# Attention scores of two light items formed in one block of matmuls, in every second slot

## What is computed

```python
# light: 8 heads of 64, windows of 64 tokens that see the window before and the window after
sim = jnp.einsum('bhnid,bhnjd->bhnij', qw * scale, kk)
sim = jnp.where(valid[None, None, :, None, :], sim, neg)
attn = jax.nn.softmax(sim, axis=-1)
lo = jnp.einsum('bhnij,bhnjd->bhnid', attn, vv)
# heavy: 256 routed queries against 256 routed keys, the same 8 heads
hsim = jnp.einsum('bhid,bhjd->bhij', hq * scale, hk)
hattn = jax.nn.softmax(hsim, axis=-1)
return light_out + heavy_out
```

## Time and profile before

| | |
|---|---|
| median of 3 runs | 2064.11 us (2062.43 to 2066.58) |
| the profiled execution's own time | 2061.01 us |
| its span, first to last instruction | 2059.2 us |
| mean granted clock of TensorE | 0.977 |
| PE busy | 1875.1 us (91%) |
| DVE busy | 1388.5 us (67%) |
| ACT busy | 1203.6 us (58%) |
| POOL busy | 1172.0 us (57%) |

### The profile page before, as it was taken

One profiled execution on the slowest core, in us unless ns is written; L12 is line 12 of the kernel. 1 busy time (PEld: TensorE's weight loads), 2 busy tenths in 40 slices (PEclk: granted clock), 3 DMA queues, 4 the chain that ended last, 5 costly groups with the idle time before them and its releaser, 6 DMA issues.

```text
span 2059.2 us, 38092 instructions
## 1 busy us (share of the span) xinstructions
PE 1875.1 (91%) x11764; PEld 1398.7 (68%) x11764; DVE 1388.5 (67%) x4771; ACT 1203.6 (58%) x2974; POOL 1172.0 (57%) x1356
## 2 busy tenths in 40 slices
PE   3488899889989989989989989989999999999998
PEld 1166678656656666666666666666666788888887
DVE  5355457756855865875874875775754488888887
ACT  5487567565565565565566566566555555555554
POOL 3999852662772782782682683583453444444444
PEclk8599999999999999999999999999999999999999
DMA  6688887200310310310310220220121111111110
GB/s 200 248 267 289 275 267 251 67 27 1 100 40 1 98 42 1 95 45 1 93 47 1 81 55 5 77 57 8 37 63 82 38 42 42 42 42 42 36 38 21
DMA packets 103841, 168.15 MB, mean 82 GB/s; under 512 B 13249, under 2 KB 64857, under 8 KB 102745
## 3 DMA queue, kind: packets, MB, share of 16 engines
q1 hardware_dynamic: 80600, 112.91, 16.8%
q0 software_dynamic: 20736, 52.52, 8.1%
q10 hardware_dynamic: 2304, 0.28, 0.1%
HBM read 80.33 MB, written 85.34 MB: 80 GB/s over the span
## 4 chain that ended last, share of the span: by engine, by line
PE 51%; DVE 16%; POOL 10%; issue 10%; ACT 9%; DMA 4%; ACTq 0%; SPq 0%; DVEq 0%; POOLq 0%
PE bank L730 7%; PE bank L732 6%; PE bank L731 6%; PE bank L1022 4%; PE bank L1011 4%; PE bank L982 4%; PE bank L993 4%; PE bank L953 3%; PE bank L890 2%; ACT prob L1319 2%; PE bank L872 2%; POOL prob L2005 2%; DVE st L1412 2%; POOL spots_d L1952 2%; PE bank L984 2%
## 5 line engine op out<-in xcount | busy, mean ns | idle before, releaser
L2005 POOL TENSOR_TENSOR prob<-prob,rden 128x512 f32<-128x512 f32 x320 | 337.6, 1056 | 453.8 <-DVE rden L1798 450.2
L1319 ACT ACTIVATE prob<-prob,nmax 128x256 f32<-128x256 f32 x512 | 256.0, 502 | 391.3 <-DVE nmax L1780 383.5
L1780 DVE CUSTOM_DVE_ANT_0 prob<-bank,mask 128x256 f32<-128x256 f32 x512 | 195.3, 417 | 103.3 <-PE bank L982 97.3
L1666 DVE SCALAR_TENSOR_TENSOR xb<-bank,gate,xb 128x256 f32<-128x256 f32 x512 | 211.8, 476 | 55.6 <-PE bank L732 55.1
L1932 POOL TENSOR_TENSOR hl<-hf,hh 128x512 fp32r<-128x512 f32 x128 | 164.7, 1291 | 113.8 <-ACT hh L1122 109.1
L982 PE MATMUL bank<-kT,qT 64*128 64x256 f32 x1024 | 211.2, 431 | 14.3 <-DVE nmax L1780 13.6
L993 PE MATMUL bank<-ident,prob 128*128 128x128 f32 x1280 | 198.8, 278 | 16.1 <-POOL prob L2005 16.1
L993 PEld LDWEIGHTS bank<-ident,prob 128*128 128x128 f32 x1280 | 154.3, 142 | 73.7 <-POOL prob L2005 26.5
L1121 ACT ACTIVATE hf<-bank,b1s 128x512 f32<-128x512 f32 x128 | 88.2, 689 | 171.2 <-PE bank L732 167.7
L1792 DVE COPY probT<-bank 128x512 f32<-128x512 f32 x160 | 110.0, 688 | 113.7 <-PE bank L993 112.8
L1011 PE MATMUL bank<-probT,V 128*64 128x128 f32 x2048 | 169.7, 287 | 9.0 <-ACT oT_s L1335 7.1
(11 more groups left out here) (256 smaller groups left out, 5044.7 us busy)
## 6 DMA issues: line engine op xcount, KB each, us to landing
xin<-spots_d SPq DMA_DIRECT2D x85, 256.0 KB
made_d<-yout SPq DMA_DIRECT2D x85, 256.0 KB
x<-in_L_attn_x SPq DMA_DIRECT2D x8, 1024.0 KB
x_d<-x SPq DMA_DIRECT2D x8, 1024.0 KB, 4.5
xb<-x_d SPq DMA_DIRECT2D x16, 512.0 KB, 3.9
out<-xb SPq DMA_DIRECT2D x16, 512.0 KB, 3.0
xb<-in_L_attn_x SPq DMA_DIRECT2D x7, 1024.0 KB, 6.7
spots_d<-zeros SPq DMA_DIRECT2D x24, 256.0 KB
```

The lines of the kernel that those rows point to most:

```text
L1319: act.activation(prob[j % NP][:, h, :], src, ACT.Exp, bias=nmax[:, j % 4, h:h + 1], scale=-1.0 if light else 1.0, accum_out=den[:, j % 4, ...
L1666: dve.scalar_tensor_tensor(out=x, in0=bank[ob][:, (t % 2) * D:(t % 2 + 1) * D], scalar=gate[:, k % 2, t, e:e + 1], in1=x, op0=ALU.mult, op ...
L1780: ins = dve.tensor_tensor_reduce(prob[j % NP][:, h, :], bank[g % NS][:, 0:KEYS], mask[:, which, :], -1.0, 3e38, ALU.add, ALU.min, nmax[:, ...
L2005: pool.tensor_tensor(prob[j % NP][:, :, :], prob[j % NP][:, :, :], rden[:, j % 4, :].unsqueeze(2).broadcast_to([P, 2, KEYS]), ALU.mult).th ...
```

## The change

`scores` is called only in the first slot of a **set**. Two light items make a set (slots 0 and 1, 2 and 3, ...), a heavy item is a set by itself. In the first slot of a set the score matmuls of both items are issued one behind the other. The first heads of both items share one bank, in its two halves of 256 columns, and the second heads share another. Three banks are still used: set n takes banks (0, 1), (2, 0) or (1, 2) in turn. PE waits once for each head of a set, on the set before and the one before that; DVE's maxima of either item wait until the matmuls of both items into that bank are done. The work itself, its shapes and its counts are the same on every engine.

```diff
+        SETS = LIGHT // 2 + SLOTS - LIGHT
+        def set_of(j):
+            b, i = divmod(j, SLOTS)
+            return SETS * b + (i // 2 if i < LIGHT else i - LIGHT // 2)
+        def set_end(n):
+            b, i = divmod(n, SETS)
+            return SLOTS * b + (2 * i + 1 if i < LIGHT // 2 else i + LIGHT // 2)
+        def score_place(j, h):
+            n, side = ((0, 1), (2, 0), (1, 2))[set_of(j) % 3][h], 0 if heavy_tile(tile_at(j)[0]) else j % 2
+            return bank[n][:, side * KEYS:(side + 1) * KEYS]
...
                 for h in range(2):
-                    g = 2 * j + h
-                    if g >= NS:
-                        if heavy_tile(tile_at((g - NS) // 2)[0]):
-                            pe.wait_ge(s_soft, g - NS + 1)
-                        else:
-                            pe.wait_ge(s_nm, g - NS + 1)
+                    old = set_end(set_of(j) - 2 + h)
+                    if old >= 0 and (j == 0 or set_of(j - 1) != set_of(j)):
+                        pe.wait_ge(s_soft if heavy_tile(tile_at(old)[0]) else s_nm, 2 * old + (1 - h) + 1)
...
-                if is_item(u):
-                    scores(u)
+                if is_item(u) and (u == 0 or set_of(u - 1) != set_of(u)):
+                    for j in range(u, set_end(set_of(u)) + 1):
+                        scores(j)
...
-                    dve.wait_ge(s_sim, g + 1)
+                    dve.wait_ge(s_sim, 2 * set_end(set_of(j)) + h + 1)
```

More of the change, by code:

```diff
@@ L65, in build @@
     NP = 4
-    NS = 3
     assert FF == P and KEYS == NSEL and HC == 4 and TG == 4 and C == 2
@@ L972, in scores @@
                 for h in range(2):
-                    g = 2 * j + h
-                    if g >= NS:
-                        if heavy_tile(tile_at((g - NS) // 2)[0]):
-                            pe.wait_ge(s_soft, g - NS + 1)
-                        else:
-                            pe.wait_ge(s_nm, g - NS + 1)
+                    old = set_end(set_of(j) - 2 + h)
+                    if old >= 0 and (j == 0 or set_of(j - 1) != set_of(j)):
+                        pe.wait_ge(s_soft if heavy_tile(tile_at(old)[0]) else s_nm, 2 * old + (1 - h) + 1)
                     hs = slice(h * DH, (h + 1) * DH)
                     if t < T:
-                        ins = pe.matmul(bank[g % NS][:, 0:KEYS], qT[hs, hp, t * P:(t + 1) * P], kT[hs, hp, t * P:t * P + KEYS], start=True, stop=True)
+                        ins = pe.matmul(score_place(j, h), qT[hs, hp, t * P:(t + 1) * P], kT[hs, hp, t * P:t * P + KEYS], start=True, stop=True)
                     else:
-                        ins = pe.matmul(bank[g % NS][:, 0:KEYS], hq[hs, hp, (t - T) * P:(t - T + 1) * P], hk[hs, hp, :], start=True, stop=True)
+                        ins = pe.matmul(score_place(j, h), hq[hs, hp, (t - T) * P:(t - T + 1) * P], hk[hs, hp, :], start=True, stop=True)
                     ins.then_inc(s_sim)
@@ L1317, in exps @@
                     act.wait_ge(s_nm, g + 1)
-                    src = prob[j % NP][:, h, :] if light else bank[g % NS][:, 0:KEYS]
+                    src = prob[j % NP][:, h, :] if light else score_place(j, h)
                     act.activation(prob[j % NP][:, h, :], src, ACT.Exp, bias=nmax[:, j % 4, h:h + 1], scale=-1.0 if light else 1.0,
@@ L1777, in maxima @@
                     g = 2 * j + h
-                    dve.wait_ge(s_sim, g + 1)
+                    dve.wait_ge(s_sim, 2 * set_end(set_of(j)) + h + 1)
                     if t < T:
-                        ins = dve.tensor_tensor_reduce(prob[j % NP][:, h, :], bank[g % NS][:, 0:KEYS], mask[:, which, :], -1.0, 3e38, ALU.add, ALU.min, nmax[:, j % 4, h:h + 1])
+                        ins = dve.tensor_tensor_reduce(prob[j % NP][:, h, :], score_place(j, h), mask[:, which, :], -1.0, 3e38, ALU.add, ALU.min, nmax[:, j % 4, h:h + 1])
                     else:
-                        ins = dve.tensor_reduce(nmax[:, j % 4, h:h + 1], bank[g % NS][:, 0:KEYS], AX_X, ALU.max, negate=True)
+                        ins = dve.tensor_reduce(nmax[:, j % 4, h:h + 1], score_place(j, h), AX_X, ALU.max, negate=True)
                     ins.then_inc(s_nm)
```

## The result

The changed kernel takes **2077.49 us** (median of 4 runs, 2074.78 to 2079.23); the kernel before, beside it, 2064.12 (2062.43 to 2066.58). The ratio is 1.007, with a 95% interval of 1.0056 to 1.0083. So the change makes the kernel 13.4 us slower, where 2054.0 us and a gain of some 10 were forecast; the time lies outside the range (2038 to 2067). The profiled execution took 2079.23 us; its attention, from the first scores to the last values, is 17.9 us longer than before's (1265.4 for 1247.5), and what lies ahead of it and behind it is equal within 0.5.

A forecast was written before the change was run, and what follows sets the result against it. PE was taken as busiest but the bound only in some slots, with DVE, POOL and ACT between. On the chain -38.3 + 28.8 gave -9.5 us, 2054.6 against the median, forecast as 2054 us, range 2038 to 2067.

The forecast's parts named there:

- What a block costs: PE's score block: 0.63 us, from two steps of passes (0.43) and one change of array shape (0.20).
- (a): 128 odd score blocks vanish: PE saves 0.20 us a set, 25.6 us in all if PE bound every slot.
- the fourth rival: Score groups: the second item's weight loads are exposed, 0.18 us net lost a set, 23 us slower, 2087; chance 0.03.
- (b): Score blocks on the chain: 56 odd ones save their piece, 67 even ones grow by 0.43 us each.
- (c): Odd pieces holding waits, as in slot 31 (0.5 us more in seven rows): the 56 sum to 38.3 us.
- (d): Sum on the chain: -38.3 + 28.8 = -9.5 us.
- (f): DVE's maxima of even items start up to 0.43 us later; slack covers it, or scores lie ready: no cost.
- (h): Whole kernel: count and size of instructions, DMAs and SP's queue don't move; a half bank reads as before, 0.41 us.
- (e): PE's waits on DVE's maxima (30.1 us, 64 cases): even slots' stay and take in PE's gain, odd slots' go.
- (g): Transposes waiting for POOL's probabilities (26.5 us, 30 cases): 0.8 us less cover, costed at nothing; 24 us if all lost it.
- The rival that ends on the other side: Even items late: slots 8 to 20 lack slack, adding 21 us, net +11.6, 2076; chance 0.10.

The follow-up runs named there:

- busy work: Kernel before, plus twelve transposes of the identity, results unread, in each of four PE waits of a row: 2056.73 us (0.9981).
- the order in slots 0 and 1: Kernel before, with DVE's rank pieces issued ahead of the reciprocals that start POOL's multiplication, in slots 0 and 1 of a row: 2059.15 us (0.9987).

## Why the prediction was wrong, step by step

- **What a block costs, and (a).** Right. Groups of eight passes take 1.06 us to the next line, and the weights are hidden: the fourth rival is out. The pairs of slots 22 to 31 alone are faster (2055.47 for 2061.90; 2047.04 for 2056.73 with busy work in both). The rows' ends gain less than was said: slots 24 to 31 are 0.6 us shorter in four of rows 0 to 6, where 1.3 was forecast, and 1.0 longer in the other three, which have halved clock there. The last pair does give 0.7; the wait ahead of slot 24 and the one in slot 28 grew.
- **(b), the hand-overs at even slots.** Right in kind: pairs 2/3 and 4/5 lose with the rank steps unchanged. The size of 0.43 us each was read from the blocks and never seen by itself; the 11 us of that run hold the clock's part as well.
- **(c), the odd pieces.** In the chain of the trace the 56 pieces sum to 40.7 us, not 38.3; with that the sum (d) would be -11.9, still further off.
- **(f), "Where DVE is behind (858 to 894) the scores lie ready anyway, and the delay costs nothing".** This step failed first. The reasoning looked only at the maxima. What comes late with PE's slot 0 is also the transposes, and with them DVE's copy; everything behind it on DVE moves against POOL, which keeps its own pace there. The run with a delay and no pair shows that 0.43 us in slot 0 alone costs 11 us.
- **(h), "The count and size of instructions ... don't move".** True, and taken to mean that their durations don't move either. The rank steps, of equal count and size, take 11 us more (104.9 for 93.9 us), nearly all of it in slots 0 to 5, where DVE is the bound. The row to see was on hand in the trace of before: a mean of 734 ns for an instruction that takes 350 alone.
- **(e), (g), waits that "take in what PE gained" or are costed "at nothing".** The transposes' waits stayed at 26.3 us in 31 cases, as forecast, but fewer and longer waits were not neutral: 14 of 20 idle times of over 1.9 us were followed by 3.4 or 6.8 us of halved clock. Halved time grew by 44 us in the attention; at half the rate that is some 22 us of work, an estimate that holds if PE is the bound in all of it. As DVE and POOL are the bound in part, it is less: work in three of its waits brought the whole change from 13.4 to 9.4 us behind before.
- **The sum (d).** Its -9.5 us did not arrive. The whole change with busy work and the order in slots 0 and 1 takes 2054.16 us, by chance the number forecast: 8.3 us under the kernel before. But busy work gives the kernel before 4.4 us and that order 3.4, each without any pair, so next to nothing is left for the pairs as a whole. The pairs of the last ten slots alone do give 9.7 us when both kernels have busy work (2047.04 for 2056.73), and those of slots 6 to 31 give 8.5 (2048.23).
- **The rivals.** The rival that ends on the other side gave 2076, near 2077.5, but for another reason: it put the loss into slots 8 to 20, and the pairs of 6 to 21 alone are faster (0.9979). The wrong place makes it a miss too. No rival had the clock or POOL's effect on DVE's durations.

The 13.4 us are accounted for in parts and not to the microsecond: the delay's loss (11 us, 7.5 with DVE's order turned in two slots, against its control) and the clock's (4 us of the whole change's) overlap, since the longer waits come with the lower clock. What the hand-overs of slots 2 and 4 cost by themselves was not separated from the clock.

## What to carry to other kernels

Saving work on the busiest engine shifts every engine behind it in time; before costing that at nothing, look at how often the instructions of the bound engine already last longer than alone (a group's mean against its shortest), and what they run beside. Here putting DVE's rank pieces ahead of the instruction that releases POOL gave 18.7 us, more than any pairing. Pair only where PE is the bound, and price a wait of PE of some 2 us at more than its length. And measure a fix in the kernel before as well: part of what it seems to mend may be a gain of its own.

## What the hardware showed that was not expected

- **DVE behind POOL.** The last rank step, an instruction of DVE with two inputs in SBUF, takes 0.34 us alone and 1.12 beside POOL's multiplication of 1.05, in five cases 1.98, and ends 0.14 to 0.16 us behind it. It looks like a wait for POOL's end, not a slower rate, since one that starts later ends at the same place. The Trainium skill states it (SBUF — State Buffer, Who interferes with whom, and Summary: rules for kernel authors): DVE and GpSimd share a port pair as an exclusive lock, an operation of DVE with two SBUF inputs contends for it with one of GpSimd that reads SBUF, and the second to issue is blocked until the first is done. The trace agrees in kind: with the order turned, all 128 of these steps are short. It holds the other way round as well: in the kernel before 11 of POOL's 320 multiplications take 1.27 to 1.31 us in place of 1.05, and each of them begins while an instruction of DVE with two SBUF inputs runs (at 880.50 POOL's L2005 takes 1.27 us, 0.11 us behind the begin of DVE's L1591, which takes 0.48). One that begins near the end of such an instruction is hardly longer (1.07 at 956.91 in the changed kernel). In the 1.98 us cases the step begins before the multiplication does by the records (855.60 and 856.37), which an overlap with it alone doesn't explain. In all five the step begins 0.25 us into POOL's DMA_INDIRECT (855.34), and the multiplication follows that at once. Rank steps beside a DMA_INDIRECT with no multiplication behind it are short (39 in the kernel before). Why the two together hold the step stays open.
- **TensorE's clock.** PE is 90% busy and more, and yet most of its idle times of over 1.9 us were followed by 3.4 us or more at a granted clock of 0.50, though PE was 95 to 100% busy in these pieces. Among the ten runs of the kernel with the last pairs alone, the two with 0.008 less of mean clock took 11 to 22 us longer than those at 0.977.
- **Useless work that pays.** 48 transposes a row of a constant tile, in waits that exist anyway, gained 4 to 8 us; where the wait had nearly gone, four added score matmuls made their block 1.72 us longer in each of seven rows.
